# Attention stage of a one-core hybrid block: choosing of experts woven into the moments, state products beside read-outs, counts at the slot's end, sends dealt out singly

## The reference, cut to what matters

```python
x = x + attn_a(layernorm(x))   # q,k = elu+1; state S += k v^T, z += k over time; o = S q / max(z.q, 1e-6); o @ W_o
x = x + ffn(layernorm(x))      # logits = x @ router_W + router_b; top-1 of 8 experts, gate = its softmax value
x = x + attn_b(layernorm(x))   # decayed running sum of x, two products, a sigmoid gate
x = x + ffn(layernorm(x))
```

## Time and profile before

| | us |
|---|---|
| median of 3 runs | 346.27 (344.2 to 346.51) |
| the profiled execution | 345.94 |
| its span | 344.1 |
| outside the span | 1.84 |
| attention's slots 2 to 7, start of `project_qk(2)` to start of slot 8 | 21.59 to 74.40 |
| first transposition of the experts on TensorE | 85.77 |
| sends of group 6 begin | 92.22 |

### The profile page before, as it was taken

How to read it: one execution, slowest core, us unless ns; L and a number is a source line. 1 busy time by engine, 2 the same in 40 slices (tenths; PEclk the granted TensorE clock), 3 DMA queues, 4 the chain that set the end, 5 groups by cost and what they waited for, 6 DMA issues and landing times.

```text
span 344.1 us, 7662 instructions
## 1 busy us (share of the span) xinstructions
PE 295.8 (86%) x2177; PEld 257.4 (75%) x2177; DVE 243.3 (71%) x1012; ACT 182.8 (53%) x545; POOL 210.9 (61%) x244
## 2 busy tenths in 40 slices
PE   7999999899976599999998997888885599999970
PEld 7566666675866599999964885766875599999970
DVE  4878998878761577777726998889573368777750
ACT  3765555321854376667613752634663376676730
POOL 4954487886485455655545857788575536565560
PEclk9999999989996899999999998999996889999995
DMA  7999211002323443221108001112313344221000
GB/s 195 257 332 144 34 40 33 31 32 58 73 63 88 94 92 91 65 57 32 32 11 236 1 1 33 40 39 71 81 41 86 93 89 104 73 55 41 31 8 1
DMA packets 32521, 25.64 MB, mean 75 GB/s; under 512 B 6000, under 2 KB 28785, under 8 KB 32480
## 3 DMA queue, kind: packets, MB, share of 16 engines
q1 hardware_dynamic: 27328, 16.51, 21.0%
q0 software_dynamic: 4576, 8.54, 7.5%
q10 hardware_dynamic: 576, 0.10, 0.2%
HBM read 14.57 MB, written 11.53 MB: 76 GB/s over the span
## 4 chain that ended last, share of the span: by engine, by line
PE 54%; POOL 10%; DVE 10%; issue 8%; ACT 6%; another core or an unknown queue 6%; DMA 1%; POOLq 0%; ACTq 0%; SPq 0%; DVEq 0%
PE pair L1498 18%; PE pair L1484 13%; POOL sorted L490 6%; PE bank L1484 6%; PE bank L1474 3%; DVE stats L797 2%; POOL rows L464 2%; PE pair L1358 2%; PE pair L1311 2%; ACT hT L741 2%; PE pair L1322 2%; PE pair L1277 1%; PE pair L1350 1%; PE pair L1333 1%
## 5 line engine op out<-in xcount | busy, mean ns | idle before, releaser
L1498 PE MATMUL pair<-w2s,hT 128*128 x624 | 87.0, 285 | 1.4 <-issue 1.1
L490 POOL DMA_INDIRECT sorted<-rows,place x64 | 67.5, 1055 | 28.2 <-issue 20.1
L1498 PEld LDWEIGHTS pair<-w2s,hT 128*128 128x128 f32 x624 | 79.6, 200 | 1.9 <-issue 1.6
L1146 DVE SCALAR_TENSOR_TENSOR ys<-pair,xs 128x128 f32<-128x128 f32 x78 | 27.3, 350 | 53.2 <-PE pair L1498 29.5
L1484 PE MATMUL pair<-xsT,w1s 128*128 128x128 f32 x432 | 61.3, 280 | 1.3 <-ACT xsT L736 1.3
L503 POOL DMA_INDIRECT x_mid<-ys,xs x39 | 41.2, 1056 | 33.2 <-DVE ys L1146 31.1
L503 POOL DMA_INDIRECT out<-ys,xs x39 | 41.1, 1055 | 33.2 <-DVE ys L1146 30.4
L1484 PEld LDWEIGHTS pair<-xsT,w1s 128*128 128x128 f32 x432 | 55.4, 196 | 2.1 <-issue 0.9
L736 ACT COPY xsT<-bank 128x128 f32<-128x128 f32 x78 | 20.8, 267 | 64.0 <-issue 34.1
L660 ACT COPY w1s<-w1all 128x516 f32 x78 | 49.5, 635 | 3.0 <-DVE etab L1074 1.9
L1484 PE MATMUL bank<-xsT,w1s 128*128 128x128 f32 x192 | 30.6, 294 | 12.9 <-ACT xsT L736 12.5
(11 more groups left out here) (164 smaller groups left out, 495.0 us busy)
## 6 DMA issues: line engine op xcount, KB each, us to landing
xs<-sorted SPq DMA_DIRECT2D x78, 66.0 KB
w1all<-in_L_ffn_W_b SPq DMA_DIRECT2D x8, 258.0 KB
rows<-in_L_attn_a_x SPq DMA_DIRECT2D x8, 256.0 KB, 4.1
w2s<-in_L_ffn_W SPq DMA_DIRECT2D x8, 256.0 KB, 6.5
rows<-x_mid SPq DMA_DIRECT2D x8, 256.0 KB, 4.3
sorted<-pad SPq DMA_DIRECT2D x30, 66.0 KB, 3.5
sorted<-rows,place POOLq DMA_INDIRECT x64
x_mid<-ys,xs POOLq DMA_INDIRECT x39
```

What stands on the lines that cost most here:

```text
L490: pool.indirect_dma_start(sorted_rows[l], bass.IndirectOffsetOnAxis(ap=place[:, t:t + 1], axis=0), rows[:, t, :], None).then_inc(s_sent[l] ...
L1146: nc.vector.scalar_tensor_tensor(out=ys[b][:], in0=bank[6 + i % 2][:, 0:P], scalar=xs[b][:, GATE:GATE + 1], in1=xs[b][:, 0:D], op0=ALU.mul ...
L1498: mm = nc.tensor.matmul(bank[6 + i % 2][:, 0:P], hT[i % NB][:, c], w2s[:, bass.ds(e, 1), c, :].rearrange("p o d -> p (o d)"), start=(c == ...
```

## The change

- **DVE.** `choose(k-2)` at the end of slot k is gone. `measure_choose_and_add_state(k-3, k-2)` in slot k takes the eight operations of group k-3 one by one between the four `bn_stats` and four `bn_aggr` of group k-2, with `add_state(k-1)` in the middle. The scores are masked before it. `phi(k)` comes before `placed(k-3)`, `scan_z(k)` after.
- **PE.** The transpositions of k are issued between the scores. `updates` and `read_intra` are one function that alternates products of both. `project_v(k)` goes before them, `count(k-3)` behind `read_inter(k-1)`. The count of group 5 goes to bank 1, and `project_out(7)` no longer waits for the places of group 5.
- **ACT.** `evac_v(k)` moves ahead, `lexp`, `row_veps` and `evac_o` move behind; `evac_o` now comes after `norm`, `row_veps` after `evac_o`.
- **POOL.** No wait for `oh`. The sends follow a list: two tiles before `row_scales` and two behind it, three tiles in slot 4.

```diff
+SENDS_OF_ATTENTION = [(range(a, b), range(b, c)) for a, b, c in
+                      ((0, 0, 0), (0, 0, 0), (0, 0, 0), (0, 0, 2), (2, 4, 5), (5, 7, 9), (9, 11, 13), (13, 15, 17),
+                       (17, 19, 21), (21, 26, 28))]
...
             for k in range(NG + 1):
...
-                after(pool, AS["oh"], k - 2)
-                if 0 <= k - 1 < NG:
+                if 0 <= k - 1:
                     z_dot_q(k - 1)
-                if k == NG:
-                    send(0, AS, k - 4, 1)
                 if k - 2 >= 0:
                     old_logits(k - 2)
+                send_tiles(0, AS, SENDS_OF_ATTENTION[k][0])
+                if k - 2 >= 0:
                     row_scales(AS, k - 2)
-                if 4 <= k < NG:
-                    send(0, AS, k - 4, 1)
-                if k - 3 >= 0:
-                    send(0, AS, k - 3, 0)
+                send_tiles(0, AS, SENDS_OF_ATTENTION[k][1])
...
+            def measure_choose_and_add_state(b, g):
+
+                sum_logits(b)
+                dve.wait_ge(AS["xnew"], g + 1)
+                row_stats(AS, g, 0)
+                scale_logits(0, AS, b)
+                row_stats(AS, g, 1)
+                bias_logits(0, AS, b)
+                row_stats(AS, g, 2)
+                max_logit(0, b)
+                row_stats(AS, g, 3)
+                lead_logits(0, AS, b)
+                if g + 1 < LASTG:
+                    add_state(g + 1)
+                dve.wait_ge(AS["st2"], 2 * g + 1)
+                row_moments(AS, g, 0)
+                rank_leaders(0, AS, b)
+                row_moments(AS, g, 1)
+                top_rank(0, b)
+                row_moments(AS, g, 2)
+                one_hot(0, AS, b)
+                row_moments(AS, g, 3)
...
                 phi(k)
+                if k - 3 >= 0:
+                    placed(0, AS, k - 3)
                 scan_z(k)
-                if k - 2 >= 0:
-                    choose(0, AS, k - 2)
...
-            def updates(g):
+            def updates_and_intra(g):
                 p = g % 2
                 n = GT if p == 0 else GT - 1
+
+                def intra(j):
+                    t = slice(j * P, (j + 1) * P)
+                    nc.tensor.matmul(bank[5][H:P, t], kv[p][:, j, VC:KC], am[:, j], start=(j == 0), stop=False,
+                                     skip_group_check=True)
+
                 pe.wait_ge(AS["kv"], g + 1)
                 after(pe, AS["state"], g)
...
                 pe.wait_ge(AS["am"], g + 1)
                 after(pe, AS["oe"], g)
                 for j in range(GT):
...
+                    if j == 1:
+                        intra(1)
+                    if j < n:
...
+                    if j != 1:
+                        intra(j)
...
-                after(pe, AS["posb"], 2 * (g - 1) - 1)
+                after(pe, AS["posb"], 2 * (min(g, LASTG - 1) - 1) - 1)
...
+                if k < NG:
+                    project_v(k)
+                if 0 <= k - 1:
+                    updates_and_intra(k - 1)
+                if 0 <= k - 1:
+                    read_inter(k - 1)
                 if 3 <= k < NG:
 
                     pe.wait_ge(AS["xnew"], k - 1)
                     count(AS, k - 3, attn_counts)
-                if 0 <= k - 1:
-                    updates(k - 1)
-                    read_intra(k - 1)
-                    read_inter(k - 1)
                 if k == NG:
-                    pe.wait_ge(AS["xnew"], k - 1)
-                    count(AS, k - 3, attn_counts)
-                if k < NG:
-                    project_v(k)
+                    count(AS, k - 3, bank[1])
```

More of the change, by code:

```diff
@@ L498, in send, with send_tiles @@
                     send_tile(l, t)
+            def send_tiles(l, S, which):
+                for t in which:
+                    if t % GT == 0:
+                        rows_ready(l, S, t // GT)
+                    send_tile(l, t)
             def scatter(l, i):
@@ L689, in attn_slot @@
                     evac_o(k - 1)
-                evac_v(k)
+                if k - 2 >= 0:
+                    row_veps(AS, k - 2)
+                if k == NG:
+                    copy_w1(0, 0)
             def gates_of_mix(g):
```

183 lines of the change are left out of this document (107 added, 76 removed).

## The result

| | before | changed |
|---|---|---|
| first comparison, median (range, executions) | 345.6 us (344.2 to 346.51, 4) | 351.77 us (349.88 to 352.61, 4) |
| ratio, 95% interval | | 1.016 [1.012, 1.020] |
| second comparison, on another chip | 317.95 (13) | 318.62 (10), 1.003 [0.999, 1.006] |
| third comparison, on a third chip | 317.39 (17) | 320.1 (6), 1.010 [1.006, 1.014] |

The changed kernel came out slower by 1.6%, 0.3% (an interval that includes no change) and 1.0%, where a gain of 1.3% was forecast. The chips differ: the kernel before takes 346 us on the first and 318 on those on which all experiments ran, and much of the difference lies in waits of the experts (DVE at the experts' results: up to 4.8 us each in the trace before of the first chip, up to 1.3 in `r0_before`).

What follows compares the result with a forecast made beforehand. TensorE held 54% of the chain, but engines took turns; POOL would be slowest (8.0 a slot). Walks plus 1.8 waits and 0.45 clock put the first transposition 4.6 us earlier; less 0.3, 345.94 became 341.6, kept as 341.7; range 339 to 346.8.

Steps and rivals of the forecast that it cites:

- DVE, choice between moments: DVE in attention: choice operations interleaved with moments save 0.75 us a slot, DVE's slot falling from 8.02 to 7.3.
- TensorE's walk: TensorE's summed operations and waits through one attention slot: forecast 7.4 us against 8.5.
- turning k between the scores: TensorE in attention: transposing k between the scores may take off 0.1 us more, or nothing.
- Updates beside read-outs: TensorE: state updates and read-outs run at once, 1.15 instead of 1.83 us; alone gives 0.04 in an even slot.
- Rival A: TensorE's updates and read-outs do not overlap; gain only 0.5 to 2 us, about 345; chance 0.13.
- TensorE, v ahead of the updates: TensorE: projecting v covers waits for kv or masked scores; the large term, 0.5 to 0.9 us a slot.
- Counts last: TensorE: count moved, not saved; in slot 8 the 0.82 wait ahead of `project_out(7)` goes, 0.4 us kept.
- The half clock can come or not: TensorE in attention: the half-clock stretch, costing about 0.9 us, may come or not; counted as 0.45.
- rival B: POOL in attention takes 8.6 us a slot or more; gain only 1 to 2.5, 343.5 to 345; chance 0.17.
- Rival C's ring: Attention: DVE's row-scales wait delays the state's copy, TensorE's read-outs, then POOL's row scales again; slower, 348; chance 0.1.
- Everything behind moves as a block: Stages behind attention keep their length and shift with it: 4.3 us earlier after 0.3 off for near misses.

Runs made afterwards that it cites:

- r0_before: The kernel before the change, run again on the chip of the experiments; 316.7 us.
- r1_changed: The changed kernel, run again beside the experiments; 318.62 us, ratio 1.003 to the kernel before.
- e3: Changed kernel with POOL's `z_dot_q(k)` moved into slot k, behind the row scales and ahead of the last sends; 316.93 us, ratio 0.998.
- d3: Changed kernel with POOL's `z_dot_q(k-1)` behind the first sends and waiting for the state of group k-1; 331.68 us, ratio 1.043.
- f2: Changed kernel with three sends ahead of the row scales and one behind, in each slot from 4 on; 318.39 us, ratio 1.003.
- r2_changed_again: The changed kernel once more, to settle its ratio; 320.1 us, ratio 1.010 to the kernel before.
- e2: Changed kernel with TensorE's updates and read-outs one after the other and k turned behind the scores, as before; 316.86 us, ratio 0.997.
- f3: Changed kernel with k turned behind the scores in slot 1 alone, plus the edits of f2 and c3; 315.77 us, ratio 0.995.
- v3: f3 with TensorE's updates and read-outs one after the other and k turned behind the scores in every slot, as e2; 315.89 us, ratio 0.992.
- c3: Changed kernel with, in slot 8, the count of group 5 behind `project_out(7)` and ACT's copy of `op` ahead of `le`; 318.51 us, ratio 1.001.
- d1: Changed kernel with unneeded products filling TensorE's idle times in slot 1, ahead of state read-outs and in slot 8; 319.12 us, ratio 1.003.
- v4: v3 with three sends a slot in slots 5 to 7, the rest behind attention, and eight filling products in slot 1; 315.64 us, ratio 0.9945.

## Why the prediction was wrong

The forecast had the first transposition 4.6 us earlier and 341.7 us as the time; it came 3.9 later on the first chip, with 351.77. r0_before and r1_changed, taken on one chip, give the balance: slots 2 to 7 gained 1.95 (48.53 against 50.48), slot 1 lost 3.51, slot 8 lost 0.93, slot 1 began 0.24 earlier, together 2.25 later. The steps of the prediction that failed are these: the cost of the choice's operations ahead of the state's copy, put at 0.11 each; slot 1, put at nothing; slot 8, put at a gain of 0.4; and the half clock, put at 0.45.

**"DVE, choice between moments: -0.75."** Right where nothing collides: slots 2, 3 and 5 took 7.1, 7.5 and 7.5 to 7.7, 0.7 to 1.4 less than before, close to the 7.4 forecast for TensorE's walk. No run tried the choice between the moments with TensorE's order of before, so this gain is that of both together. The step failed in that it put five of the choice's eight operations ahead of TensorE's state and priced them at 0.11 without asking what POOL does meanwhile. I read from the trace of before that the choice's operations took 0.19 and never that they lay beside POOL's sends there, while its product lay beside the moments, which is where the change puts the choice. Where the two meet ahead of the state's copy, one operation takes 1.3 to 1.9, and slot 4 takes 8.4. Shown by e3, d3 and f2: with the product elsewhere slot 4 takes 7.27, 7.36 and 7.24.
The Trainium skill, SBUF — State Buffer, Who interferes with whom, says that a DVE instruction with two SBUF inputs contends with a GpSimd instruction that reads SBUF. The traces agree: `lsum` 1.27 to 1.55 where `z_dot_q` starts beside it, 0.17 to 0.20 away from it.
How much of the whole loss is of this kind is not shown: e3 and f2 free single slots and move the collision into others, and d3 pays elsewhere.

**Slot 1, not in the sum.** The prediction started its walk at slot 2 and let "turning k between the scores" take off 0.1 or nothing. The change also moved `setup_transposes` behind a wait, and slot 1 lost 1.3 us at full clock (9.61 in f2 against 8.32) and 1.9 to 3.5 with the clock. In r1_changed and r2_changed_again this is the largest single loss (on the first chip the turn behind slot 8 lost 2.89, most of it at half clock), and the diff showed it: a call that stands between two halves of a function that became one.

**"Updates beside read-outs."** The forecast of next to nothing was right where four updates stand (7.56 and 7.54 in slot 3, r1_changed and e2). Where three stand, some 0.25 was forecast and 0.08 came (7.10 and 7.18 in slot 2). f3 against v3 confirms it for the total. Rival A, which denied the overlap, is refuted, and its reading of the trace of before ("only one place") was too narrow: read-outs start ahead of earlier updates in slots 1, 5, 7 and 8. v3 shows why interleaving by hand adds nothing. Its read-outs stand behind the updates in the program and overlap them all the same, since the masked scores are ready in time.

**"TensorE, v ahead of the updates", 0.5 to 0.9 a slot.** The waits that it was to cover are gone, but no run tried it alone. In r0_before the waits for kv are 0.22 to 0.33, not 0.6 to 0.9 as in slots 4, 5 and 7 of the first chip, so there was less to cover on the later chips.

**"Counts last", 0.4 kept in slot 8.** The choice of group 5 moved into slot 8 with the rest of the interleaving, so the wait for the places became one of 1.57 for the one-hot rows, ahead of `project_out(7)`: slot 8 takes 0.9 to 1.8 more instead of 0.4 less. c3 gets back 0.76.

**"The half clock can come or not: 0.45."** The term was too small: on the first chip 17.1 us of attention ran at half speed where before had 3.4. On the chips of the experiments before has a median clock of 0.977 to 0.982 and the changed kernel 0.966 and 0.956. What that costs can be read from the executions of one kernel, as a coincidence of clock and time and no more: three of v3 at a mean clock of 0.987 took 312.7 to 313.3, five at 0.961 to 0.962 took 316.7 to 317.2, so 1.6 us for 0.01. The slope over all executions of before is 1.6 to 2.0, over those of d1 and v4 only 0.5 to 0.7. With 1.6, and reduced to 0.978, r1_changed would take 316.7 and r2 316.6, a third of a per cent under before: an estimate. By it, the change shortens the walks by little, makes TensorE idle in longer pieces (up to 1.60 instead of 0.91), and loses the gain by the clock. d1, the run that tried this, brought the clock back in attention and no time (1.003), so that account stays unproven.

**POOL, rival B.** The first send came at 39.80, not at 41.2. In the changed kernel POOL idles 0.8 to 2.1 a slot ahead of its row scales and bounds nothing. In f2, f3 and v3, where three sends stand ahead of the row scales, POOL has no such idle time in slots 5 to 7 and needs 8.2 to 8.3 from product to product, about what slots 5 and 6 take; there rival B's walk fits. v4's slots 5 and 6 are as long with POOL idle, so it is not the only bound. Rival C's ring appeared in e3 only. The prediction erred to the slower side, and none of its rivals had the mechanism.

**"Everything behind moves as a block."** Held on the later chips: r1_changed is 2.25 behind r0_before at the first transposition and 2.4 at the end. On the first chip the 3.9 grew to 6.8 within the second experts, whose code is the same, at waits of 2 to 5.4 us (DVE at the experts' results) that only that chip shows. What makes these waits, and whether the growth is the change's, stays open; so does how much of the 1.016 is.

## What to carry to other kernels

Before operations are interleaved, ask for each what ran on the neighbouring engine at its old place and what will at its new one: an operation's length in the trace holds for its old neighbours only. When two functions are merged, look at what stood between them, and who waits for it. And a change that gathers TensorE's short waits into long ones may have to be charged for the clock: here mostly 1.2 to 2.0 us for each 0.01 of mean clock, as far as clock and time go together, which is as much as the walks had to give.
